# Attention groups of a twelve-stage decoder kernel: the transfers of the maxima rows issued by ScalarE instead of the sync engine

## The chip, the cores and the metric

The kernel is one program on one core of a Trainium2 chip. The metric is the device time of one execution in microseconds (us). The core has four compute engines, each with an instruction queue of its own: TensorE (PE in the profile), VectorE (DVE), ScalarE (ACT) and GpSimd (POOL). A fifth, the sync engine (SP), computes nothing and issues transfers. The engines meet only at semaphores. An engine takes its own queue in order, so whatever stands behind a wait waits too.

## The reference

The model is a decoder of four layers with three stages each, on x of 8 sequences, 256 positions and 128 features. Each stage adds f(layernorm(x)) to x. Five of the twelve stages are softmax attention with 16 heads of 8 features, and they are all that the change touches:

```python
# x: (8, 256, 128); L0a and L1a: self-attention with rotary q and k, causal
# L0x, L1x, L3x: cross-attention, keys and values from ctx_1024 (8, 256, 128)
Q, K, V = split_heads(q @ Wq + bq), split_heads(k @ Wk + bk), split_heads(v @ Wv + bv)
scores = jnp.einsum('bhqd,bhkd->bhqk', Q, K) / jnp.sqrt(8)      # causal or masked, but not in L3x
attn = jax.nn.softmax(scores, axis=-1)
attn = attn * group_prob[:, None]                               # L0x alone
x = x + jnp.einsum('bhqk,bhkd->bhqd', attn, V).merge_heads() @ Wo + bo
```

The stages run in the order L0a, L0x, L0f, L1a, L1x, L1f, L2a, L2x, L2f, L3a, L3x, L3f.

## The kernel before, in words

One function, `attention`, runs a whole group of attention stages as one pass: L0a with L0x, L1a with L1x, and L3x by itself. A pass works on items, one for each pair of stage and sequence: 16, 16 and 8 items, 40 in all. Below, items are counted from 0 to 39 over the three passes (0 to 7 are L0a, 8 to 15 L0x, 16 to 23 L1a, 24 to 31 L1x, 32 to 39 L3x).

The order of all work is written out by hand in slots. `PER` is 16 slots for each item, and the step of item i with offset `off` is done in slot 16 i + off. Each engine's program walks through the same slots and issues what falls into each, in the order of its own code. Many items are in flight at once.

What one item does, as far as it matters here:

- Slots 0 to 15: TensorE makes the scores q by k for each of 8 pairs of heads and two halves of the queries (`scores`, L714). VectorE takes each row's maximum over the keys (`row_max`, L962 and L965) into `mx`.
- Slot 16 (`MAX_CUT`): GpSimd cuts each maximum into three bf16 parts, so that a matmul can bring it in without loss (`cut_max`, L537 to L540).
- Slot 18 (`MT`): TensorE turns the parts (`turn_max`, L669). Slot 19: ScalarE copies them from PSUM to the one buffer `mT` (L890), which raises `mT_ready`.
- Slot 20 (`MAX_IN`): the sync engine waits for `mT_ready` and issues two transfers, each of 64 rows of 512 bytes, from `mT` into the operand `Qm` (L490). They raise `max_in0` or `max_in1`, by turns. ScalarE's next copy into `mT`, an item later, waits for them.
- Slots 24 to 39: TensorE makes the scores again, now keys by queries with the maxima rows as part of the operand (`keyed_scores`, L736, followed in some stages by L738 or L741 for masks). In slot 24, v = 0, it waits for both transfers. ScalarE takes the exponential in the same slot (L839) into a ring of 8 buffers `Pr`, and TensorE multiplies by the values in groups of four slots (`times_v`, L766). The keyed scores have two PSUM banks, so that TensorE in slot n waits for the exponential of slot n - 2.

So slots 16 i + 16 to 16 i + 23 of item i hold the keyed scores and exponentials of item i - 1, v = 8 to 15. In slot 20 ScalarE has the exponential with v = 12 of the item before and, for most items, one small exponential of a layernorm (L863).

The sync engine's other work in the same stretch, in the order of its code: in slot 19 the loads of the first half of the operands of item i + 2 (`stack_in`, L448: two into `Kst`, two into `Qm`, each waiting for its image in device memory); in slot 20, for L0x items, a load of the gate `G` (L474); then `MAX_IN`; in slot 21 the three writes of the k parts of item i + 3 to its image (`parts_out`, L440; 3, 2 and 1 parts of 64 KB). Masks are loaded at L465. In the first two passes GpSimd issues transfers of its own near slots 18 and 21: zeros to a buffer in device memory (L573, first pass alone) and half an expert's weights (L1500).

In slot 21 ScalarE also makes the first part of q of item i + 3 for cross-attention (`first_part`, L829), and VectorE takes the rest in slot 22 (`take_rest`, L928).

Of the kernel before, what the change touches and what calls it, by code (L numbers as in the profile page):

```python
# [36 lines left out]
DEPTH = 3  # L37
# [140 lines left out]
def load_next_weights(core, sp):  # L178

    if core.at + 1 < len(STAGES):  # L180
        st = STAGES[core.at + 1]
        sp.dma_start(core.stage_W[(core.at + 1) % 2][:, 0:width(WEIGHTS[st])], core.dram[f"small_{st}"])\
            .then_inc(core.sem["stage_w"], 16)
# [15 lines left out]
def end_pass_sync(core, sp, kind):  # L199

    sp.wait_ge(core.sem["iter_done"], 4)
    for name in ALL_STAGES + PASS_SEMS[kind]:
        sp.sem_clear(core.sem[name])  # L203
    for go in ("go_pe", "go_act", "go_dve", "go_pool"):
        sp.sem_inc(core.sem[go], 1)
# [87 lines left out]
def attention(core, sts):  # L293

    nc, s, PS, w = core.nc, core.sem, core.PS, core.w
# [18 lines left out]

    STATS, AGGR, VAR, LN, EXP, NORM = -48, -47, -46, -45, -44, -43
    XT, K, Q, V, MT, SEL, AT, Y = -38, -34, -28, 8, 18, 45, 49, 55
    MAX_CUT, MAX_IN = 16, 20
    K_CUT, Q_CUT, K_OUT, Q_OUT = -31, -25, -27, -21
    STACK_IN, FIRST_STACK_IN = (-13, -7), {"k": -22, "q": -20}
    MASK_IN, NEG, GATE_IN, XB, FFN_IN, ZERO_IN = -23, -7, 4, 45, 5, 2  # L320
# [12 lines left out]
    def slot_of(i, off):  # L333
        return PER * i + off - (LEAD[off][i] if i < 3 and off in LEAD else 0)

    def at(n, off):
        return next((i for i in range(N) if slot_of(i, off) == n), None)
# [4 lines left out]
    def unit(n, off, span=PER):  # L342
        i, r = divmod(n - off, PER)
        return (i, r) if 0 <= i < N else (None, 0)
# [3 lines left out]
    def gates(i, v, pool):  # L348
        return (10 if pool else 6) * (i - gated_from) + sum(1 for x in range(v + 1) if on_pool(x) == pool)

    def stack_slot(i, half, what):
        if i >= DEPTH:
            return PER * i + STACK_IN[half]
        return FIRST_STACK_IN[what] if i == 0 else PER * i + FIRST_STACK_IN["q"] - LEAD[Q][i]
# [5 lines left out]
    with ExitStack() as c:  # L360
# [7 lines left out]
        Qm, vaug = core.Qm, core.vaug  # L368
# [10 lines left out]
        mT = sb("mT", [P, S], BF16)  # L379
# [38 lines left out]
        with nc.Block() as block:  # L418

            @block.sync  # L420
            def _(sp):
                if first:
                    first_loads(core, sp)
                load_next_weights(core, sp)

                def parts_out(i, what, ready):

                    sp.wait_ge(s[ready], i + 1)
                    if i >= 2:
                        for half in range(2):  # L430
                            sp.wait_ge(s[f"{what}_stack{(i - 2) % DEPTH}_{half}"], 32 * ((i - 2) // DEPTH + 1))
                    out = image[what][i % 2].rearrange("s r t -> r s t")
                    if what == "k":
                        runs = ((0, 3, part["k"][:, 0:3, :]), (3, 2, part["k"][:, 0:2, :]), (5, 1, part["k"][:, 0:1, :]))
                    else:
                        three = part["q"][:, 0:1, :].broadcast_to([P, 3, S])
                        runs = ((0, 3, part["q"][:, 0:3, :]), (3, 2, part["q"][:, 0:2, :]), (5, 1, part["q"][:, 0:1, :]))
                        runs = ((0, 3, three), (3, 2, part["q"][:, 1:2, :].broadcast_to([P, 2, S])), (5, 1, part["q"][:, 2:3, :]))
                    for slot, n, src in runs:
                        sp.dma_start(out[:, slot:slot + n, :], src).then_inc(s[f"{what}_image{i % 2}"], 16)  # L440

                def stack_in(i, half, what):
                    buf, pairs = i % DEPTH, slice(half * HP // 2, (half + 1) * HP // 2)
                    sp.wait_ge(s[f"{what}_image{i % 2}"], 48 * (i // 2 + 1))
                    for par in range(2):
                        rows = image[what][i % 2].rearrange("s (r d p) t -> r s d p t", r=2, d=DH)[par][:, :, pairs, :]
                        to = Kst[64 * par:64 * par + 64, buf, pairs] if what == "k" else Qm[64 * par:64 * par + 64, buf, par, pairs]
                        sp.dma_start(to.rearrange("p h t -> p (h t)"), rows.rearrange("s d p t -> s d (p t)"))\  # L448
                            .then_inc(s[f"{what}_stack{buf}_{half}"], 16)

                for n in SLOTS:
                    i = at(n, K_OUT)
                    if i is not None:
                        parts_out(i, "k", "k_parts")
                    i = at(n, Q_OUT)
                    if i is not None:
                        parts_out(i, "q", "q_parts")
                    i = at(n, MASK_IN)
                    if i is not None and items[i][0] in MASKED:
                        st, b = items[i]  # L460
                        m = i - masked_from
                        if m > 0:
                            sp.wait_ge(s["neg_ready"], m)
                        for k in range(2):
                            sp.dma_start(msk[:, k, :, :], core.dram[f"mask{st[1]}" + "qk"[k]][b]  # L465
                                         .rearrange("(t p) k -> p t k", p=P)).then_inc(s["mask_in"], 16)
                    i = at(n, GATE_IN)
                    if i is not None and items[i][0] in GATED:
                        st, b = items[i]
                        m = i - gated_from  # L470
                        if m >= DEPTH:
                            sp.wait_ge(s["pg_dve"], gates(i - DEPTH, PER - 1, False))
                            sp.wait_ge(s["pg_pool"], gates(i - DEPTH, PER - 1, True))
                        sp.dma_start(G[:, i % DEPTH], core.dram["gate_prob"][b].rearrange("(t p) k -> p t k", p=P))\  # L474
                            .then_inc(s[f"gate_in{m % DEPTH}"], 16)
                    for half in range(2):
                        for what in "kq":
                            i = next((j for j in range(N) if stack_slot(j, half, what) == n), None)
                            if i is not None:
                                if i >= DEPTH:  # L480
                                    sp.wait_ge(s["st_psum"], PER * (i - DEPTH) + 8 * (half + 1))
                                if i == 0:
                                    sp.wait_ge(s["image_set"], 16 * 6)
                                    sp.wait_ge(s["setup"], set_up)
                                stack_in(i, half, what)
                    i = at(n, MAX_IN)
                    if i is not None:
                        sp.wait_ge(s["mT_ready"], i + 1)
                        for par in range(2):
                            sp.dma_start(Qm[64 * par + 56:64 * par + 64, i % DEPTH, par].rearrange("c p t -> c (p t)"),  # L490
                                         mT[64 * par:64 * par + 64, :]).then_inc(s[f"max_in{i % 2}"], 16)
                    if second and n == PER * (second - 1) + Y + 1:
                        sp.wait_ge(s["x_done"], second)
                        core.at += 1
                        load_next_weights(core, sp)
                        core.at -= 1
                end_pass_sync(core, sp, "attention")
                nxt = core.at + len(sts)
                sp.wait_ge(s["stage_w"], 16 * nxt)
# [320 lines left out]
            def _(act):  # L820
# [23 lines left out]
                for n in SLOTS:  # L844
# [4 lines left out]
                    i, v = unit(n, TLAG)  # L849
                    if i is not None:  # L850
                        exponentials(i, v)
                    i = at(n, LN)
# [5 lines left out]
                    i = at(n, EXP)  # L858
# [5 lines left out]
                    i = at(n, NORM + 1)  # L864
# [8 lines left out]
                    i = at(n, XT + 1)  # L873
# [5 lines left out]
                    i = at(n, K + 1)  # L879
                    if i is not None and items[i][0] not in ROPE:  # L880
                        first_part(i, "k", f_bank(K))
                    i = at(n, Q + 1)
                    if i is not None and items[i][0] not in ROPE:
                        first_part(i, "q", f_bank(Q))
                    i = at(n, MT + 1)
                    if i is not None:
                        act.wait_ge(s["mT_psum"], i + 1)
                        if i > 0:
                            act.wait_ge(s[f"max_in{(i - 1) % 2}"], 32 * ((i - 1) // 2 + 1))
                        a(mT[:, :], PS[:, f_bank(MT), 0:P].bitcast(BF16), ACT.Copy).then_inc(s["mT_ready"], 1)  # L890
                    i = at(n, AT + 1)
                    if i is not None:
                        act.wait_ge(s["aT_psum"], i + 1)
# [3 lines left out]
                    i, x = unit(n, PV_LAG + 5)  # L897
# [1684 lines left out]
```

## Time and profile before

| | |
|---|---|
| time before, median of 3 runs | 1683.09 us (1681.88 to 1686.23) |
| the profiled execution, its own time | 1681.12 us |
| span of its instructions | 1679.0 us |
| mean granted TensorE clock | 0.865 of full speed |
| busy: TensorE, VectorE, ScalarE, GpSimd | 1244.2, 981.0, 640.0, 574.5 us |

The profile is of one execution. Its span runs from the first instruction to the end of the last; the program's own time holds 2.12 us more, and is 1.97 us below the median of the three runs. Busy time of an engine is not the same as time that it sets: an engine can be idle because it waits for another, and in another stage it can be the one waited for. Transfers that the sync engine or ScalarE issues are counted at the issuing queue (SPq), and what they take to land is to be read from who waits for them.

### The profile page before, as it was taken

To read this page: it belongs to the slowest core of one execution; us is meant where nothing else is said; L and a number is where in the kernel's file an instruction comes from. 1 tells how busy PE (TensorE), PEld (TensorE's weight loads), DVE (VectorE), ACT (ScalarE), POOL (GpSimd) and SP (SyncE) were. 2 spreads that over 40 slices of the span, in tenths; PEclk is the share of its full clock that TensorE was granted. 3 is DMA by queue.
4 is the path that set the end of the run, shared out by engine and by line. 5 is a ranking of instruction groups with operands and counts; after the bars stand their busy time and mean duration, and the time that the engine had idled before them with its cause. 6 is when DMAs were issued, how large, how long until landed. Compare 5 with 4: busy or idle time off the path is not lost. (4 is left out here: it accounts for less than half of the span.)

```text
span 1679.0 us, 30784 instructions
## 1 busy us (share of the span) xinstructions
PE 1244.2 (74%) x9153; PEld 792.0 (47%) x9153; DVE 981.0 (58%) x4171; ACT 640.0 (38%) x1532; POOL 574.5 (34%) x1102
## 2 busy tenths in 40 slices
PE   4688889995293589999963947649488738995686
PEld 2455555552283356555533936538244424543232
DVE  5666777764775677787726735566333428863332
ACT  1344544542032156566541424214123314763221
POOL 3543478873332444455203433134100012310000
PEclk8899999997596699999985968859689969997888
DMA  5544654510111434554201140111100034310000
GB/s 181 162 130 141 192 170 140 159 35 15 32 56 60 149 111 137 163 166 136 76 10 40 57 152 1 44 42 55 43 0 0 0 101 131 120 48 1 0 0 25
DMA packets 139962, 137.80 MB, mean 82 GB/s; under 512 B 12240, under 2 KB 109136, under 8 KB 139552
## 3 DMA queue, kind: packets, MB, share of 16 engines
q1 hardware_dynamic: 131200, 111.40, 21.5%
q0 software_dynamic: 8608, 24.55, 4.6%
q8 instruction: 72, 1.18, 0.3%
q14 instruction: 82, 0.67, 0.1%
HBM read 84.10 MB, written 49.18 MB: 79 GB/s over the span
## 5 line engine op out<-in xcount | busy, mean ns | idle before, releaser
L839 ACT ACTIVATE L0a_Pr<-PS 128x512 f32<-128x512 f32 (+1 forms) x256 | 137.3, 547 | 153.5 <-PE PS L741 88.0
L839 ACT ACTIVATE L1a_Pr<-PS 128x512 f32<-128x512 f32 (+1 forms) x256 | 136.1, 547 | 104.8 <-PE PS L741 52.5
L557 POOL TENSOR_TENSOR L0a_PG<-L0a_Pr,L0a_G 128x512 f32<-128x512 f32 x80 | 105.8, 1327 | 29.5 <-ACT L0a_Pr L839 13.7
L962 DVE CUSTOM_DVE_ANT_0 L1a_junk<-PS,L1a_neg 128x256 bf16<-128x256 f32 x256 | 94.8, 420 | 33.7 <-PE PS L714 33.3
L962 DVE CUSTOM_DVE_ANT_0 L0a_junk<-PS,causal_q 128x128 bf16<-128x128 f32 (+1 forms) x256 | 78.5, 352 | 53.5 <-PE PS L714 52.7
L736 PE MATMUL PS<-Qm,L0a_Kst 128*128 128x512 bf16 (+1 forms) x256 | 93.2, 364 | 22.3 <-DMA Qm<-L0a_mT 19.2
L714 PE MATMUL PS<-L0a_Kst,Qm 128*128 128x256 bf16 (+1 forms) x512 | 95.1, 273 | 17.6 <-DVE L0a_mx L962 10.6
L714 PE MATMUL PS<-L1a_Kst,Qm 128*128 128x256 bf16 (+1 forms) x512 | 94.5, 271 | 16.1 <-DVE L1a_mx L962 9.2
L962 DVE CUSTOM_DVE_ANT_0 L1a_junk<-PS,causal_q 128x128 bf16<-128x128 f32 (+1 forms) x256 | 78.5, 352 | 37.4 <-PE PS L714 36.8
L736 PE MATMUL PS<-Qm,L1a_Kst 128*128 128x512 bf16 (+1 forms) x256 | 91.3, 357 | 10.8 <-DMA Qm<-L1a_mT 7.5
L965 DVE TENSOR_REDUCE L3x_mx<-PS 128x2 f32<-128x512 f32 x128 | 83.8, 686 | 22.4 <-PE PS L714 22.1
L962 DVE CUSTOM_DVE_ANT_0 L0a_junk<-PS,L0a_neg 128x256 bf16<-128x256 f32 x192 | 72.8, 418 | 35.6 <-PE PS L714 35.0
L839 ACT ACTIVATE L3x_Pr<-PS 128x512 f32<-128x512 f32 x128 | 73.1, 602 | 35.6 <-PE PS L736 35.1
L714 PEld LDWEIGHTS PS<-L0a_Kst,Qm 128*128 128x128 bf16 x512 | 44.5, 103 | 62.2 <-DVE L0a_mx L962 32.1
L714 PEld LDWEIGHTS PS<-L1a_Kst,Qm 128*128 128x128 bf16 x512 | 43.8, 102 | 60.6 <-DVE L1a_mx L962 30.4
L738 PE MATMUL PS<-neg_k,ident_b 128*128 128x256 bf16 x256 | 71.8, 280 | 0.0
L766 PE MATMUL PS<-L1a_Pr,vaug 128*32 128x256 f32 (+1 forms) x1024 | 61.7, 358 | 0.2 <-ACT L1a_Pr L839 0.2
L714 PE MATMUL PS<-L3x_Kst,Qm 128*128 128x256 bf16 x256 | 51.4, 286 | 13.9 <-DVE L3x_mx L965 9.3
L736 PE MATMUL PS<-Qm,L3x_Kst 128*128 128x512 bf16 x128 | 47.8, 381 | 5.9 <-ACT L3x_Pr L839 5.1
L741 PE MATMUL PS<-L0a_neg,ident_b 128*128 128x512 bf16 x128 | 48.5, 379 | 0.0
L741 PE MATMUL PS<-L1a_neg,ident_b 128*128 128x512 bf16 x128 | 48.5, 379 | 0.0
L2010 POOL COPY L3a_dAb<-L3a_dA 128x1024 f32<-128x1024 f32 x4 | 4.2, 1042 | 128.3 <-DVE L3a_dA L2153 128.3
(722 smaller groups left out, 3255.5 us busy)
## 6 DMA issues: line engine op xcount, KB each, us to landing
Qm<-q_image SPq DMA_DIRECT2D x160, 128.0 KB
sorted_in<-zeros POOLq DMA_DIRECT2D x16, 516.0 KB, 4.3
L0a_Kst<-k_image SPq DMA_DIRECT2D x64, 128.0 KB
ffn_w_<-L_ffn POOLq DMA_DIRECT2D x32, 256.0 KB, 4.0
L1a_Kst<-k_image SPq DMA_DIRECT2D x64, 128.0 KB
ffn_w_<-L_ffn SPq DMA_DIRECT2D x16, 256.0 KB, 7.1
L3x_Kst<-k_image SPq DMA_DIRECT2D x32, 128.0 KB
k_image<-L0a_kpart SPq DMA_DIRECT2D x16, 192.0 KB
```

The lines of the kernel that those rows point to most:

```text
L557: g.tensor_tensor(PG[:, V_ % GATED_RING, :].rearrange("p (h q) -> p h q", h=2), Pr[:, V_ % RING, :].rearrange("p (h q) -> p h q", h=2), G[ ...
L714: ins = mm(PS[:, bank, par * nk:(par + 1) * nk], Qm[:, buf, par, hp, tt * P:(tt + 1) * P], Kst[:, buf, hp, 0:nk], start=(par == 0), stop=T ...
L736: ins = mm(o, Kst[:, buf, hp, kt * P:(kt + 1) * P], Qm[:, buf, :, hp, q0:S], start=True, stop=True, **free)
L738: ins = mm(o[:, :, 0:P], core.ident_b[:, :], core.neg_k[:, :].unsqueeze(1).broadcast_to([P, 2, P]), start=False, stop=True, **free)
L741: ins = mm(o, core.ident_b[:, :], neg[:, buf, 1, kt].unsqueeze(1).broadcast_to([P, 2, S]), start=False, stop=True, **free)
L766: ins = mm(o, vaug[:, buf, half, kt, 4 * g + j, :], src[:, par * nq:(par + 1) * nq], start=(kt == 0 and half == 0), stop=True, **free)
L839: a(Pr[:, V_ % RING, 0:2 * nq], PS[:, T_BANK + v % 2, 0:2 * nq], ACT.Exp, scale=SCALE)\
L962: ins = v.tensor_tensor_reduce(junk[:, tt, par, 0:nk], scored[:, par], off, 1.0, LOWEST, ALU.add, ALU.max, mx[:, i % 2, tt, par, hp:hp + 1])
L965: ins = v.tensor_reduce(mx[:, i % 2, tt, :, hp:hp + 1], scored, AX, ALU.max)
L2010: g.tensor_copy(dAb[:, :, :, :], dA[:, :, :].unsqueeze(3).broadcast_to([P, T, NH, P]))\
```

## The change

The step `MAX_IN` of the sync engine is taken out. Its wait and its two transfers, unchanged, go into ScalarE's program, in slot MT + 2 = 20, behind that slot's exponential(s) and ahead of slot 21's. Nothing else is touched: same transfers, same semaphores, same slot number.

```diff
-    MAX_CUT, MAX_IN = 16, 20
+    MAX_CUT = 16
...
-                    i = at(n, MAX_IN)
-                    if i is not None:
-                        sp.wait_ge(s["mT_ready"], i + 1)
-                        for par in range(2):
-                            sp.dma_start(Qm[64 * par + 56:64 * par + 64, i % DEPTH, par].rearrange("c p t -> c (p t)"),
-                                         mT[64 * par:64 * par + 64, :]).then_inc(s[f"max_in{i % 2}"], 16)
...
                         a(mT[:, :], PS[:, f_bank(MT), 0:P].bitcast(BF16), ACT.Copy).then_inc(s["mT_ready"], 1)
+                    i = at(n, MT + 2)
+                    if i is not None:
+                        act.wait_ge(s["mT_ready"], i + 1)
+                        for par in range(2):
+                            act.dma_start(Qm[64 * par + 56:64 * par + 64, i % DEPTH, par].rearrange("c p t -> c (p t)"),
+                                          mT[64 * par:64 * par + 64, :]).then_inc(s[f"max_in{i % 2}"], 16)
```

## Rows read from the trace of the kernel before

**Rows 1.** Busy us by stretch (L0a, L1x, L3x): stretch, length, engines, clock, DMA share, GB/s

```profile
66.00:186.00 120.00, 99.75 (x937) 63.31 (x935) 76.60 (x464) 59.31 (x153) 53.22 (x134) 0.93 0.47 145
...
716.00:838.00 122.00, 119.90 (x1022) 67.61 (x1021) 92.82 (x491) 74.37 (x162) 51.54 (x96) 1.00 0.42 128
1413.00:1507.00 94.00, 89.67 (x803) 49.38 (x802) 71.38 (x143) 65.06 (x142) 21.61 (x68) 1.00 0.30 93
```

**Rows 2.** Line L736 on TensorE: its idle time before it by what ended it, us, times

```profile
  DMA Qm<-L0a_mT: 19.2, 8
  DMA Qm<-L1a_mT: 7.5, 7
...
  DMA Qm<-L3x_mT: 0.7, 1
```

**Rows 3.** Line L490, the sync engine's issues: ns min/median/max, first and last start

```profile
L490 SPq DMA_DIRECT2D Qm<-L0a_mT x32: 608/654/954, 55.1 to 371.5; - x32
```

**Rows 4.** Timeline of item 23 (L1a): start us, us, engine, line, [idle before <-releaser]

```profile
696.93 0.38 ACT L890 ACTIVATE L1a_mT<-PS 128x256 bf16<-128x256 bf16 x1
...
699.64 1.34 SPq L490 DMA_DIRECT2D Qm<-L1a_mT  x2
...
702.88 0.39 PE L736 MATMUL PS<-Qm,L1a_Kst 128*128 128x512 bf16 x1 [2.20 <-DMA Qm<-L1a_mT]
```

**Rows 5.** Timeline of item 29 (L1x)

```profile
806.43 0.38 ACT L890 ACTIVATE L1a_mT<-PS 128x256 bf16<-128x256 bf16 x1
...
807.67 1.34 SPq L490 DMA_DIRECT2D Qm<-L1a_mT  x2
...
812.12 0.39 PE L736 MATMUL PS<-Qm,L1a_Kst 128*128 128x512 bf16 x1 [1.47 <-DMA Qm<-L1a_mT]
```

**Rows 6.** Timeline of item 8 (L0x): the sync engine's queue and TensorE

```profile
208.87 0.45 SPq L474 DMA_DIRECT2D L0a_G<-gate_prob  x1
...
209.40 1.35 SPq L490 DMA_DIRECT2D Qm<-L0a_mT  x2
...
216.08 0.39 PE L736 MATMUL PS<-Qm,L0a_Kst 128*128 128x512 bf16 x1 [3.27 <-DMA Qm<-L0a_mT]
```

**Rows 7.** Busy us by stretch: item 8's issue to its use

```profile
209.40:216.10 6.70, 3.42 (x37) 2.12 (x36) 4.12 (x19) 2.79 (x9) 3.43 (x10) 1.00 0.96 283
```

**Rows 8.** Timeline of item 2 (L0a): all transfers issued from 89.07 on, and TensorE

```profile
89.07 1.20 SPq L448 DMA_DIRECT2D Qm<-q_image  x2
...
92.59 0.72 POOL L573 DMA_DIRECT2D sorted_in<-zeros  x1
92.89 1.34 SPq L490 DMA_DIRECT2D Qm<-L0a_mT  x2
...
98.18 0.57 PE L736 MATMUL PS<-Qm,L0a_Kst 128*128 128x512 bf16 x1 [2.22 <-DMA Qm<-L0a_mT]
```

**Rows 9.** Timeline of item 35 (L3x), the stretch around slots 19 to 24

```profile
1446.68 0.38 ACT L890 ACTIVATE L3x_mT<-PS 128x256 bf16<-128x256 bf16 x1
...
1447.09 1.34 SPq L490 DMA_DIRECT2D Qm<-L3x_mT  x2
1447.21 0.61 ACT L839 ACTIVATE L3x_Pr<-PS 128x512 f32<-128x512 f32 x1
1447.69 0.22 ACT L863 ACTIVATE L3x_r<-L3x_lnv 128x2 f32<-128x2 f32 x1
1447.78 0.62 ACT L839 ACTIVATE L3x_Pr<-PS 128x512 f32<-128x512 f32 x1
...
1448.26 0.51 ACT L829 ACTIVATE L3x_qpart<-PS,stage_W 128x256 bf16<-128x256 f32 x1
1448.54 1.46 SPq L440 DMA_DIRECT2D k_image<-L3x_kpart  x3
...
1449.43 0.38 PE L736 MATMUL PS<-Qm,L3x_Kst 128*128 128x512 bf16 x1
...
1450.31 0.38 PE L736 MATMUL PS<-Qm,L3x_Kst 128*128 128x512 bf16 x1
```

## The prediction

> **What bounds the kernel now.** I read the busy times by stretch first. In the attention passes TensorE is the engine that sets the pace: it is busy for 99.75 of 120 us in L0a (83%), 119.90 of 122 in L1x (98%) and 89.67 of 94 in L3x (95%), with ScalarE at 49%, 61% and 69% [rows 1]. The reader is to see that ScalarE has room on average, and that in L1x and L3x there is next to no idle time of TensorE left to win.
>
> Then I read what TensorE waits for at the line that uses the moved transfers, L736. It waits for them in 16 of 40 items: 19.2 us in eight items of the first pass, 7.5 in seven of the second, 0.7 in one of L3x, 27.4 us in all [rows 2]. That is the ceiling of any gain. The other 24 items use rows that have landed in time, or so nearly that no wait of note is shown.
>
> Then I read timelines, to see whether such a wait is the sync engine's lateness, the transfer's own time, or queueing. Three kinds show up.
>
> In item 23 the copy ends at 696.93 + 0.38 = 697.31, but the sync engine issues at 699.64, 2.33 us late. TensorE goes on at 702.88, 3.24 us after the issue, with 2.20 us of wait [rows 4]. In item 29 the issue is 807.67 - 806.81 = 0.86 us late, and the wait 1.47 [rows 5]. I took these starts for all 40 items: only these two issue more than 0.1 us behind the copy.
>
> In item 8 the issue is prompt, but the gate's load, issued at 208.87, stands ahead of it in the sync engine's queue. The rows are used 6.68 us after the issue, with 3.27 us of wait [rows 6], while the DMA engines are 96% busy [rows 7].
>
> In item 2 the last transfers ahead of it in that queue were issued at 89.07 and 1.20 on, over 2.6 us before the issue at 92.89. Still the rows are used only 5.29 us after it. What was issued close by is GpSimd's 92.59 [rows 8].
>
> Against these stands the landing with little in its way: at most 1450.31 - 1447.09 = 3.22 us in item 35 [rows 9], and 3.24 in item 23.
>
> **The change part by part.** Removed from the sync engine: 40 waits and 80 issues, of about 0.65 us each [rows 3], some 52 us of its queue. Added to ScalarE: the same.
>
> *Gain 1, the late issues.* ScalarE issues behind its own copy, so items 23 and 29 are no longer late. Item 23 gives back its whole 2.20 us (2.33 earlier). Item 29 gives 0.86 to 1.47; I take 1.0. Sum 3.2 us.
>
> *Gain 2, item 8.* In a queue of its own the transfer isn't behind the gate's load. Bounds 0 and 3.27 us. I take 2.0, because the DMA engines stay as full and GpSimd's transfers are still there.
>
> *Gain 3, the other waits.* In the first pass they are 19.2 - 3.27 = 15.9 us, in the second 7.5 - 2.2 - 1.5 = 3.8, in L3x 0.7. They could all go (20.4) or none. I take 1.5, by item 2, the plainest row: its own queue was clear, and the 2.05 us beyond 3.24 went to another engine's transfers. Another queue doesn't remove those.
>
> *Cost 1, the image writes move up.* With the wait for `mT_ready` gone, the sync engine goes straight to slot 21's three writes of the k parts, 384 KB (6 parts of 64 KB). In item 35 they are issued at 1448.54, directly behind the maxima's 1.34 us [rows 9]; now they start as early as or earlier than the maxima's, and compete. At the 283 GB/s seen in a full stretch [rows 7], 384 KB are 1.4 us, the most that they can put ahead; the least is 0. If the two queues share, each byte of the maxima's 64 KB waits for one of the image, 0.23 us. I take that, for the 14 items that wait and weren't late: 14 x 0.23 = 3.2 us. The 24 without a wait have slack.
>
> *Cost 2, ScalarE's queue.* Behind the two issues stand slot 21's exponential, the first part of q and slot 22's exponential; TensorE waits for the exponentials two slots on, VectorE for q. In item 35 the two issues would occupy the queue from 1447.09 to 1448.43 [rows 9]. The exponential and layernorm step of slot 20 (1447.21 and 1447.69) stand ahead of them in program order. I take it that these are already handed to the arithmetic and run on meanwhile: ScalarE's rows overlap, the next starting before the last has ended (1447.21 + 0.61 is after 1447.69), so instructions are taken ahead of the work. Then slot 21's exponential starts at 1448.43 instead of 1447.78 and ends at 1449.05, and TensorE's matmul that needs it starts at 1449.43: 0.38 us to spare. The first part of q ended at 1448.26 + 0.51 = 1448.77; 0.65 us later and with slot 22's exponential of 0.62 us behind it, that is 1450.04, before slot 24's matmul at 1450.31, which waits for it. Cost nothing, the cover being that two-slot lag. Without it, up to 0.65 us an item.
>
> The Trainium skill's page "Advanced Engine Details and Errata", section "Sequencer Loop", speaks of such a queue: engine instructions are pushed into a queue, and run on while the sequencer executes a control instruction. By it this cost is nothing, where an issue that holds up the arithmetic costs what rival A has; no row here shows ScalarE issuing a transfer.
>
> The sum: -3.2 - 2.0 - 1.5 + 3.2 + 0 = -3.5 us. Span 1679.0 - 3.5 = 1675.5. The profiled execution's own time is 2.1 more and its distance to the median 2.0, so the median goes from 1683.1 to 1679.6 us, 0.2% less. About 0.3%, 5 us, is what a measurement of this kernel can tell from no change. The forecast's own range, with gain 2 between 0 and 3.3, gain 3 between 0 and 6 and cost 1 between 0 and 6, is 1674 to 1685.
>
> **The rivals.**
>
> *A. The issue isn't hidden behind ScalarE's work (slower).* If the two issues start only when slot 20's work is done, they start in item 35 at 1447.69 + 0.22 = 1447.91, 0.82 us late. The landing, 3.22 later, is at 1451.13, 0.82 us behind today's use, and slot 21's exponential ends at 1449.25 + 0.62 = 1449.87, 0.44 us behind the matmul that needs it. The place is slot 24's matmul, the price about 0.6 us (less in items without the layernorm step), in the 14 waiting items and some 12 of L1x and L3x with under 0.5 us of slack: 26 x 0.6 = 15.6 us. Against the -3.5 that is +12: 1695 us. It decides from a delay of 0.2 us on, L3x's slack. For it speaks that no row shows such an issue; against it, the overlapping rows. A partial form, 0.3 us an item, gives +4: 1687.
>
> *B. A queue of its own removes most queueing (faster).* If the DMA engines serve a third queue's small transfers ahead of what GpSimd and the sync engine have waiting, gain 3 is two thirds of its 20.4, 13.6 us, and gain 2 is 3.3, cost 1 nothing: -20 us, 1663. A half-way form gives 1671. For it speaks item 8; against it item 2.
>
> *C. Nothing comes of it (the same).* The transfers land as they did except for the two late ones, and the image writes take back those 3.2 us: 1683. Items 2 and 35 speak for it.
>
> A rule of the Trainium skill speaks for C: "DMA: Bandwidth & Descriptors", section "Issuing engines are not separate DMA queues", says that transfers of all issuers run on the same 16 DMA engines and interleave, and that several issuers save only the time of issuing. Item 2's 5.29 us, with nothing ahead in its queue, agree. By it gains 2 and 3 would be nothing, and the sum 0.
>
> **How the numbers follow.** Chances: the forecast 0.48, A 0.21, B 0.13, C 0.18. Below 1678.0 is faster, above 1688.1 slower. Of the forecast, 0.20 fall below 1678 and 0.27 between, 0.01 above. Of A, 0.17 are slower and 0.04 same. B is faster. C is 0.02 faster, 0.14 same, 0.02 slower. That makes faster 0.35, same 0.45, slower 0.20. The range takes in the forecast's own, C, the half-way form of B and the partial form of A up to some 0.4 us an item: 1670 to 1690. Outside lie the full B (0.07) and the full A (0.11).
>
> **What the profile after would show.** Right: ScalarE's queue issues within 0.1 us of the copy's end in all 40 items, items 23 and 29 lose their waits, item 8's falls under 1.5 us, TensorE's total wait for these rows is 20 to 25 us, and TensorE's waits for ScalarE's exponentials at L736 stay about as they are. The image writes are issued before or beside the maxima's. Wrong by A: issues 0.3 us or more behind the copy, new waits in L3x, exponentials of slot 21 that end after their matmul could start. Wrong by B: the total wait under 12 us. The prediction would also fail if an issue on ScalarE takes much longer than 0.65 us, for then the two slots no longer cover it.

## The result: slower, outside the predicted range

| | before | after |
|---|---|---|
| median, runs side by side on one chip | 1683.09 us (1680.24 to 1686.82, 5 runs) | 1708.81 us (1704.42 to 1716.94, 5 runs) |
| ratio after to before, 95% interval | | 1.0131 [1.0104, 1.0159] |
| the profiled execution, own time | 1681.12 us | 1716.94 us |

The change costs 25.7 us in the median. The prediction was 1679.6 with a range to 1690. The profiled execution of the changed kernel is the longest of its five, 8.1 us above their median, so its parts are first sorted by place. In the changed kernel the lines stand six lower: L736 is L730, L839 is L833, L890 is L884; ScalarE's new issues are L889.

The page of the changed kernel, its span, its busy times and two of its DMA queues:

```profile
span 1715.1 us, 30784 instructions
...
PE 1267.3 (74%) x9153; PEld 808.3 (47%) x9153; DVE 980.3 (57%) x4171; ACT 638.0 (37%) x1532; POOL 572.8 (33%) x1102
...
q1 hardware_dynamic: 125440, 108.78, 20.9%
...
q10 hardware_dynamic: 5760, 2.62, 0.6%
```

The work is the same, and q10 is a queue that the page of before doesn't have: 2.62 MB, which are 80 transfers of 64 rows of 512 bytes. ScalarE's transfers do have a queue of their own.

The stretches from the first item's copy into `mT` to the last item's, for each of the three passes (stretch, length, busy us of TensorE, its weight loads, VectorE, ScalarE and GpSimd, TensorE's clock, DMA share, GB/s). Before:

```profile
55.12:370.85 315.73, 281.52 (x2695) 170.82 (x2694) 224.07 (x1061) 156.49 (x369) 203.63 (x353) 0.97 0.46 143
577.94:842.68 264.74, 247.85 (x2247) 147.67 (x2246) 197.26 (x1116) 155.25 (x369) 116.22 (x254) 0.99 0.42 131
1400.03:1508.21 108.18, 101.44 (x888) 54.66 (x886) 82.30 (x168) 74.25 (x163) 25.86 (x82) 1.00 0.30 92
```

After:

```profile
55.29:382.22 326.93, 286.82 (x2694) 173.14 (x2693) 223.55 (x1061) 155.70 (x369) 203.08 (x353) 0.95 0.45 138
588.03:860.39 272.36, 249.35 (x2247) 147.59 (x2246) 196.64 (x1116) 154.41 (x369) 116.06 (x254) 0.98 0.42 126
1426.96:1539.31 112.35, 103.77 (x888) 56.20 (x886) 82.23 (x168) 74.13 (x163) 25.88 (x82) 0.97 0.30 90
```

The passes are longer by 11.2, 7.6 and 4.2 us, 23.0 together, of which 13.9 are idle time of TensorE (length less busy: 34.2, 16.9 and 6.7 became 40.1, 23.0 and 8.6) and 9.1 are the same matmuls taking longer. The profiled span is 36.1 us longer, and the rest lies where nothing was edited: 9.2 us between the second and the third pass (566.57 against 557.35, at a clock of 0.77 instead of 0.79) and 5.0 behind the last copy (175.8 against 170.8, at 0.82 instead of 0.84), less 1.1 us elsewhere. The four other executions have spans of 1702.5 to 1707.1 us, so they hold little of this. I put the change's cost at the 23 to 26 us that passes and medians show.

TensorE's waits for the moved transfers (total, times, longest), to be held against [rows 2]:

```profile
PE PS L730 <- DMA Qm<-L0a_mT: 23.7, 8, 3.8
PE PS L730 <- DMA Qm<-L1a_mT: 14.0, 12, 2.4
...
PE PS L730 <- DMA Qm<-L3x_mT: 3.0, 3, 2.5
```

They were 27.4 us in 16 items and are 40.7 in 23. That is 13.3 of the 13.9 us of idle time. TensorE's wait for exponentials of the first pass at the same line rose from 3.1 to 4.8 us, in the two later passes it stayed (3.1 and 5.1).

ScalarE's new issues, ns min/median/max:

```profile
L889 ACTq DMA_DIRECT2D Qm<-L0a_mT x32: 623/625/2373, 55.3 to 382.9; - x32
L889 ACTq DMA_DIRECT2D Qm<-L1a_mT x32: 623/624/1131, 588.1 to 861.1; - x32
L889 ACTq DMA_DIRECT2D Qm<-L3x_mT x16: 623/624/1139, 1427.0 to 1540.0; - x16
```

The median is that of the sync engine [rows 3]; the maximum isn't.

Item 21 shows what happens. It is an item that hardly waited before (timeline; start, us):

```profile
664.86 0.38 ACT L890 ACTIVATE L1a_mT<-PS 128x256 bf16<-128x256 bf16 x1
...
665.26 1.34 SPq L490 DMA_DIRECT2D Qm<-L1a_mT  x2
...
666.72 2.52 SPq L440 DMA_DIRECT2D k_image<-L1a_kpart  x3
...
668.44 0.39 PE L736 MATMUL PS<-Qm,L1a_Kst 128*128 128x512 bf16 x1
```

The same item after:

```profile
677.12 1.43 SPq L440 DMA_DIRECT2D k_image<-L1a_kpart  x3
...
677.96 0.38 ACT L884 ACTIVATE L1a_mT<-PS 128x256 bf16<-128x256 bf16 x1
...
678.37 0.62 ACTq L889 DMA_DIRECT2D Qm<-L1a_mT  x1
...
678.59 0.47 SPq L465 DMA_DIRECT2D L1a_msk<-mask1q  x1
...
679.02 0.73 ACTq L889 DMA_DIRECT2D Qm<-L1a_mT  x1
679.10 0.94 SPq L465 DMA_DIRECT2D L1a_msk<-mask1k  x1
...
680.91 1.22 SPq L448 DMA_DIRECT2D L1a_Kst<-k_image  x2
682.23 1.19 SPq L448 DMA_DIRECT2D Qm<-q_image  x2
...
683.85 0.39 PE L730 MATMUL PS<-Qm,L1a_Kst 128*128 128x512 bf16 x1 [2.41 <-DMA Qm<-L1a_mT]
```

Before, the sync engine stood in front of its wait for `mT_ready` until the copy ended, and everything behind that wait came after the maxima. After, three image writes are issued 1.22 us before the copy ends (677.12 against 678.34), the two mask loads come between and beside ScalarE's issues, and four operand loads follow before the rows are used. The rows are used 5.51 us after the copy (683.85 - 678.34) instead of 3.20 (668.44 - 665.24). The prediction's list of what moves up had the image writes alone; the masks and the operand loads were missing.

### The profile page after: what moved, and what is told of

It is laid out like the page before. It is cut to its first block and busy times, and to the rows that moved or that the text cites. A ratio compares the mean times of both kernels' runs of the same rounds, so it can differ in the third digit from the quotient of the medians.

```text
span 1715.1 us, 30784 instructions
## 1 busy us (share of the span) xinstructions
PE 1267.3 (74%) x9153; PEld 808.3 (47%) x9153; DVE 980.3 (57%) x4171; ACT 638.0 (37%) x1532; POOL 572.8 (33%) x1102
## 3 DMA queue, kind: packets, MB, share of 16 engines
q10 hardware_dynamic: 5760, 2.62, 0.6%
## 5 line engine op out<-in xcount | busy, mean ns | idle before, releaser
L833 ACT ACTIVATE L0a_Pr<-PS 128x512 f32<-128x512 f32 (+1 forms) x256 | 136.8, 546 | 172.0 <-PE PS L735 89.8
L833 ACT ACTIVATE L1a_Pr<-PS 128x512 f32<-128x512 f32 (+1 forms) x256 | 135.8, 547 | 120.5 <-PE PS L732 63.5
L730 PE MATMUL PS<-Qm,L0a_Kst 128*128 128x512 bf16 (+1 forms) x256 | 94.5, 369 | 28.5 <-DMA Qm<-L0a_mT 23.7
L730 PE MATMUL PS<-Qm,L1a_Kst 128*128 128x512 bf16 (+1 forms) x256 | 91.6, 358 | 17.3 <-DMA Qm<-L1a_mT 14.0
L962 DVE CUSTOM_DVE_ANT_0 L0a_junk<-PS,L0a_neg 128x256 bf16<-128x256 f32 x192 | 72.7, 418 | 36.5 <-PE PS L708 36.1
L833 ACT ACTIVATE L3x_Pr<-PS 128x512 f32<-128x512 f32 x128 | 73.1, 601 | 40.5 <-PE PS L730 40.2
L730 PE MATMUL PS<-Qm,L3x_Kst 128*128 128x512 bf16 x128 | 49.1, 391 | 8.2 <-ACT L3x_Pr L833 5.1
```

Source lines behind the costliest of these rows:

```text
L730: ins = mm(o, Kst[:, buf, hp, kt * P:(kt + 1) * P], Qm[:, buf, :, hp, q0:S], start=True, stop=True, **free)
L833: a(Pr[:, V_ % RING, 0:2 * nq], PS[:, T_BANK + v % 2, 0:2 * nq], ACT.Exp, scale=SCALE)\
L962: ins = v.tensor_tensor_reduce(junk[:, tt, par, 0:nk], scored[:, par], off, 1.0, LOWEST, ALU.add, ALU.max, mx[:, i % 2, tt, par, hp:hp + 1])
```

## The experiments

Each is compared with the kernel before, run on the same chip in between (medians 1686.4 to 1687.2 us). "Landing" is the time from the end of item i's copy to the semaphore update of the second transfer, read from each trace; the means are over the eight items 1 to 8 and the seven items 33 to 39. Before, they are 5.50 and 3.03 us; in the changed kernel 6.36 and 3.12. Waits and landings are those of one profiled execution of each kernel.

The expectations name theories by letters. W: the sync engine's transfers, no longer held back, are what costs. Q: ScalarE's queue is served worse. E: ScalarE's exponentials come late. S: the transfers of two issuers at one time delay each other. D: it is the bytes, from whichever queue. G: the loss needs GpSimd's transfers as a third party.

| kernel | time, us | ratio, 95% interval | waits for the rows | landing 1–8 | 33–39 |
|---|---|---|---|---|---|
| changed + sync waits for the copy | 1705.79 | 1.0112 [1.0092, 1.0131] | 40.4 | 6.45 | 3.19 |
| changed + sync waits for the landing | 1684.71 | 0.9989 [0.9971, 1.0007] | 26.1 | 5.51 | 3.02 |
| before, image writes first | 1715.32 | 1.0166 [1.0140, 1.0192] | 50.6 | 6.33 | 3.34 |
| before + spares on ScalarE | 1717.57 | 1.0183 [1.0163, 1.0204] | 54.0 | 6.34 | 4.14 |
| before + one-row spares on ScalarE | 1692.03 | 1.0036 [1.0008, 1.0063] | 32.6 | 5.59 | 3.17 |
| before + spares two slots later | 1685.52 | 1.0002 [0.9979, 1.0025] | 27.3 | 5.51 | 3.06 |
| before + spares on the sync engine | 1694.81 | 1.0051 [1.0027, 1.0074] | 32.4 | 5.64 | 3.13 |
| before, GpSimd's transfers moved | 1658.42 | 0.9821 [0.9799, 0.9843] | 10.4 | 3.67 | 3.04 |
| changed, GpSimd's transfers moved | 1668.23 | 0.9882 [0.9851, 0.9914] | 16.4 | 4.04 | 3.01 |
| the same + sync waits for the landing | 1656.35 | 0.9813 [0.9787, 0.9839] | 11.6 | 3.90 | 3.02 |

### The changed kernel, with the sync engine held until the copy

```diff
+                    i = at(n, MT + 2)
+                    if i is not None:
+                        sp.wait_ge(s["mT_ready"], i + 1)
```

> The changed kernel, but the sync engine still waits for the maxima's copy in slot 20 before it goes on to the image writes; it issues nothing there. Theory W (the k parts' image writes, which the old wait held back until after the maxima's issues, now go first and fill the DMA engines): the writes can start at the copy's end at the earliest, so that items 21, 22, 32 and those of L1x, where they moved up by 1.2 us and more ahead of the copy, get their landing back to within 0.5 us of before, and items 1 to 4 and 17 to 20, where they moved to about the copy's end in any case, stay. About a third to a half of the loss comes back: 1695 to 1700 us. Theory Q (ScalarE's queue is served worse than the sync engine's, whatever else goes on): nothing comes back, 1705 to 1712 us. Theory E (ScalarE's exponentials come late): nothing comes back either.

It keeps the wait in the sync engine's program and leaves the transfers on ScalarE, so the image writes start 0.03 us after the copy's end, at the same moment as ScalarE's issues. 1705.79 us: it gives back little, less than the third to a half that theory W had forecast. In the first two passes, what goes *beside* the maxima in another queue costs as much as what goes ahead of them (landings of 6.45 us in items 1 to 8 against 6.36). L3x gets its time back, with waits of 1.0 us where the changed kernel has 3.0.

L3x also shows how little the image writes cost by themselves. In items 33 to 36 of this run nothing but the three image writes, 384 KB, is issued by the sync engine from the copy's end until 2.78 us after it, and they start at the same moment as ScalarE's issues. The rows land 3.09, 3.53, 3.32 and 3.31 us after the copy, on the mean 0.28 us later than before the change. (Item 32, the first of the pass, lands 1.1 us later; its second issue is late too.) The same writes beside them go with 0.95 us in items 1 to 8, where GpSimd's transfers are on their way too.

### The changed kernel, with the sync engine held until the landing

```diff
+                    i = at(n, MT + 2)
+                    if i is not None:
+                        sp.wait_ge(s[f"max_in{i % 2}"], 32 * (i // 2 + 1))
```

> The changed kernel, but the sync engine waits in slot 20 until the maxima's transfers have landed, so that no image write is issued while they are on their way. Theory W: landings as before the change or better, TensorE's wait for these rows at or below the 27 us of before, 1675 to 1684 us. Theory Q: landings stay late in busy stretches, 1700 us or more. Theory E: no change, 1705 to 1712 us. If the writes come too late for the loads that need them, new waits for the stacks at L708 would show.

The transfers are still issued by ScalarE, in its queue, in all 40 items. The waits (this kernel's L733; L3x no longer appears):

```profile
PE PS L733 <- DMA Qm<-L0a_mT: 19.2, 8, 3.8
...
PE PS L733 <- DMA Qm<-L1a_mT: 6.9, 9, 2.2
```

The whole loss is gone: 1684.71 us, a ratio of 0.9989 with an interval that holds 1. So neither ScalarE's issuing nor its queue costs the time by itself; the sync engine's transfers do that it no longer holds back. This is the run that settles the main cause, although the time is 0.7 us above the range of theory W. It doesn't tell image writes from masks and loads, since it holds all of them. It also holds them longer than the kernel before did, until the landing and not only until the issue, and no run holds the kernel before for as long; a small cost of ScalarE's issues that this makes up for isn't excluded here.

### The kernel before, with the image writes ahead in the same queue

```diff
-                    i = at(n, K_OUT)
-                    if i is not None:
-                        parts_out(i, "k", "k_parts")
...
+                    i = at(n + 1, K_OUT)
+                    if i is not None:
+                        parts_out(i, "k", "k_parts")
                     i = at(n, MAX_IN)
```

> The kernel before, with the sync engine's three image writes of the k parts put ahead of the maxima's wait and transfers instead of behind them; ScalarE issues nothing. It is the change's second effect, the writes moved up, without its first, the other issuer. Theory W (the moved writes are what costs): the rows land about 1.3 us later where the k parts are ready just before the copy (L0a, L1a), less in L1x and L3x; the wait at L736 grows from 27 to 45 us or more, 1700 to 1712 us. Theory S (what costs is that two engines issue at one time, whatever they issue): one queue, so no more than the issues' own delay, about 0.6 us in items 1 to 8 and 17 to 24, 1688 to 1697 us.

Item 3 of it:

```profile
118.21 0.38 ACT L890 ACTIVATE L0a_mT<-PS 128x256 bf16<-128x256 bf16 x1
...
118.38 1.43 SPq L440 DMA_DIRECT2D k_image<-L0a_kpart  x3
...
119.86 2.12 SPq L490 DMA_DIRECT2D Qm<-L0a_mT  x2
...
124.72 0.39 PE L736 MATMUL PS<-Qm,L0a_Kst 128*128 128x512 bf16 x1 [3.04 <-DMA Qm<-L0a_mT]
```

With ScalarE out of it altogether, the order alone costs 28.2 us (1715.32 against 1687.16), 3 us more than the range of theory W and far from that of theory S. Here a part of the price is plain to see as a late issue: 119.86 is 1.27 us after the copy's end. Counted from its own first issue the transfer takes no longer than before in items 1 to 8 (5.47 us on the mean against 5.48). From the copy's end it is 6.33, against 6.36 in the changed kernel, where the issue is prompt and the transfer is longer. In the first pass the writes that go ahead cost 0.83 to 0.86 us an item, whether the maxima stand behind them in one queue or share the DMA engines with them from another.

### Spare transfers on ScalarE, on the sync engine, smaller, and later

The kernel before keeps its order, and ScalarE issues two more transfers of the same 64 rows into a tile that nobody reads, in slot 20; ScalarE's next copy into `mT` waits for them too.

```diff
+                    i = at(n, MT + 2)
+                    if i is not None:
+                        act.wait_ge(s["mT_ready"], i + 1)
+                        for par in range(2):
+                            act.dma_start(spare[64 * par + 56:64 * par + 64].rearrange("c p t -> c (p t)"),
+                                          mT[64 * par:64 * par + 64, :]).then_inc(s["dum_in"], 16)
```

> The kernel before, with two more transfers of the same size and source issued by ScalarE in slot 20, into a spare buffer that nobody reads; the real ones stay with the sync engine. It adds the occupation of ScalarE's queue (80 issues) and 64 KB an item, and leaves the image writes where they were. Theory E (the issues on ScalarE cost by themselves): slower by 10 us or more. Theory W: within 0.3% of before, 1679 to 1688 us, the real rows landing up to 0.2 us later. Theory Q says nothing of it, but the spare transfers' landings would be late.

1717.57 us, as slow as the changed kernel and more. That is what theory E had forecast and theory W hadn't. Item 37 lies in a stretch of L3x in which no other transfer is issued until 2.78 us after the copy:

```profile
1506.99 0.38 ACT L892 ACTIVATE L3x_mT<-PS 128x256 bf16<-128x256 bf16 x1
...
1507.39 1.34 SPq L491 DMA_DIRECT2D Qm<-L3x_mT  x2
1507.40 0.65 ACTq L897 DMA_DIRECT2D L3x_spare<-L3x_mT  x1
1508.08 0.62 ACTq L897 DMA_DIRECT2D L3x_spare<-L3x_mT  x1
...
1511.43 0.39 PE L737 MATMUL PS<-Qm,L3x_Kst 128*128 128x512 bf16 x1 [0.65 <-DMA Qm<-L3x_mT]
```

The real rows, issued 0.02 us after the copy's end, are used 4.06 us after it. With no spares they land 3.04 us after it. So 64 KB more, started at the same moment by another engine, put 1.0 us onto a transfer that has the DMA engines nearly to itself otherwise.

Most of that isn't time in which the rows' data are moved. By the trace's records of single packets, the last data packet of the real rows ends 2.69, 2.70 and 2.29 us after the copy in items 37 to 39, where it ended at 2.29, 2.31 and 2.23 before. The last semaphore update comes 1.33, 1.60 and 1.58 us behind that packet, and came 0.75, 0.74 and 0.73 us behind it before. No run shows what fills that time.

This run alone can't say whether ScalarE's 1.3 us of issuing has a part in it. The same two transfers in slot 22 (`MT + 4` in place of `MT + 2`) answer that:

> The two whole spare transfers on ScalarE again, issued in slot 22 instead of 20, some 2 us after the real ones. Theory S: the real rows are issued and nearly landed by then, landing in L3x back to 3.0 us, and the time within 0.5% of before, 1680 to 1693 us; what stays comes from the image writes and loads behind. Theory E: as slow as with slot 20, or slower, since the exponential of slot 23 is nearer to its use: 1710 us or more.

```profile
1482.11 0.38 ACT L892 ACTIVATE L3x_mT<-PS 128x256 bf16<-128x256 bf16 x1
...
1482.52 1.34 SPq L491 DMA_DIRECT2D Qm<-L3x_mT  x2
...
1483.74 1.30 ACTq L897 DMA_DIRECT2D L3x_spare<-L3x_mT  x2
...
1485.74 0.38 PE L737 MATMUL PS<-Qm,L3x_Kst 128*128 128x512 bf16 x1
```

ScalarE's queue is held for the same 1.3 us, the real rows land after 3.06 us again, and the kernel takes 1685.52 us, no more than before (the interval reaches to 0.25%, 4 us). TensorE's waits for exponentials at the line of the keyed scores are 2.1 us longer than before, 13.4 against 11.3, but a cost of ScalarE's queue time can't be told in the kernel's time. Theory E, which had 1710 us or more here, falls.

The spares cut to one row of 512 bytes each (`spare[64 * par + 56:64 * par + 57, 0, :]` from `mT[64 * par:64 * par + 1, :]`):

> As the run with two spare transfers on ScalarE, but each moves one row of 512 bytes instead of 64. Theory S by descriptors (the making of the descriptors of both issuers' transfers is one shared step, whose time goes with their number): the real rows land as before the change, in L3x 3.0 us after the copy, and the time is within 0.3% of before, 1680 to 1690 us. Theory S by transfers (a fixed time for each transfer): the landing stays at 4.0 us, and 1705 to 1718 us. Theory E (ScalarE's queue is what costs): the exponentials come late as with the whole spare transfers only if an issue still takes 0.6 us.

1692.03 us, 2 us above the forecast range, and landings of 3.1 to 3.2 us in L3x. The number of transfers is the same, so most of the cost goes with what is in them. The 4.9 us that are left weren't followed up.

And the full spares issued by the sync engine, right behind the real ones:

> The same two spare transfers, issued by the sync engine directly behind the real ones: same bytes, one queue. Theory S: the real rows' landing stays within 0.2 us of before (3.0 in L3x), 1680 to 1692 us. Theory D (it is the bytes on the DMA engines that delay, from whichever queue): landings 0.3 us and more later, over 1695 us.

1694.81 us, with 3.1 to 3.2 us in L3x. The landing is what theory S had forecast, the time is 3 us above its range, and the waits are 5 us longer than before; the sync engine is busy with 80 more issues, and which of its later work comes late by them wasn't looked into.

Behind in the same queue, the same bytes cost the real rows 0.1 us; beside them in another queue, 1.0. But that is not the queue alone. Behind the real ones, the spares are issued 1.4 us after the copy. The spares two slots later are in the other queue and are issued 1.25 us after the copy (1483.74 against 1482.49), and they cost the rows nothing either. In L3x, then, what protects the rows is the head start of some 1.3 us. One queue gives it by its order, since the two issues ahead take 0.65 us each. In two queues that wait for the same copy it is gone.

### GpSimd's transfers out of the way

What made items of the first pass wait in the kernel before? GpSimd's zeros and weights were moved in their slots, with and without the change:

```diff
-    MASK_IN, NEG, GATE_IN, XB, FFN_IN, ZERO_IN = -23, -7, 4, 45, 5, 2
+    MASK_IN, NEG, GATE_IN, XB, FFN_IN, ZERO_IN = -23, -7, 4, 45, 14, 12
```

> The kernel before, with GpSimd's two transfers of an item (zeros, half an expert's weights) issued in slots 12 and 14 of an item instead of 2 and 5, which are slots 18 and 21 of the item before. If the waits for the maxima rows before the change were queueing behind these, most of the 27.4 us of wait go: TensorE's wait at L736 for the rows under 10 us in all, and 1655 to 1668 us. If they only move the collision to the operand loads of slots 3 and 9, waits for the stacks at L714 grow and the time stays at 1675 to 1690 us.

```profile
PE PS L736 <- DMA Qm<-L1a_mT: 5.0, 5, 2.4
...
PE PS L736 <- DMA Qm<-L0a_mT: 4.5, 4, 1.9
...
PE PS L736 <- DMA Qm<-L3x_mT: 0.9, 1, 0.9
```

1658.42 us, 28.0 us less than the kernel before beside it, within the forecast range, and waits of 10.4 us instead of 27.4. The first pass is 22.4 us shorter (293.36 against 315.73). Items 2 to 5 land after 3.05 to 3.09 us. Most of the queueing that the change was up against was GpSimd's, and a change of issuer didn't touch it.

> The changed kernel with GpSimd's transfers of the two items of pass 1 moved twelve and ten slots on, as in the run of the kernel before with the same move (1658.4 us). Theory W (the changed kernel lets the sync engine's image writes go ahead of the maxima's transfers, and theory S, that the two issuers' transfers delay each other) has nothing to do with GpSimd: the change should cost here what it cost in the kernel before, 15 to 25 us on top of 1658.4, so 1673 to 1685 us, with landings at 4 to 6 us after the copy in most items. Rival G (the loss needs GpSimd's transfers as a third party): the change costs under 5 us here, 1655 to 1663 us, landings near 3.1 us.

(The moves are nine slots for the weights and ten for the zeros, as the diff has them, and not the twelve and ten of the text above.) With the change on top it is 1668.23 us. The change costs 9.8 us here instead of 25.7 (10.4 by the two ratios, as the two kernels ran on different chips), less than either way of 15 to 25 that I had expected, and more than 5. Landings in items 1 to 8 are 0.37 us later than without the change, where they were 0.86 later with GpSimd's transfers in place. So the sync engine's transfers cost some time by themselves, and more where three engines' transfers meet.

> The changed kernel in which the sync engine waits for the landing of the maxima's transfers before it goes on, with GpSimd's transfers moved as well. By theory W nothing of the sync engine's overlaps the maxima's transfers, so landings are 3.0 to 3.2 us after the copy in nearly all items, the late issues of items 23 and 29 are gone too: 1650 to 1660 us. If holding the sync engine for some 3 us an item makes its own image writes and loads late once the queueing is gone, it is 1660 to 1672 us, with waits for K or V images among those of TensorE.

1656.35 us, which can't be told from the 1658.42 without the change: the intervals of their ratios overlap almost wholly. Item 23 lost most of its late issue's wait (1.85 us became 0.14), but items 24 and 29 wait 1.88 and 1.70 us in its place. No form of the change was shown to gain anything; moving GpSimd's transfers alone was.

## Why the prediction was wrong

**The step that failed is Cost 1.** It named the right mechanism, with an upper bound, and then took 0.23 us for 14 items, 3.2 us. Measured: the waits rose by 13.3 us, though items 23 and 29 gave back 0.70 and 1.47, so the others lost 15.5. Three things were wrong in it.

- *The price by bytes.* 64 KB at 283 GB/s are 0.23 us. That is near what the image writes cost in the quiet stretch of L3x (0.28 us, the run in which the sync engine waits for the copy), but only one of the 14 priced items, item 32, lies in L3x. The mean over items 1 to 8 of the changed kernel was 0.86, and with GpSimd's transfers moved 0.37. Nor is it a price for all transfers: the spares put 64 KB beside the rows and cost 1.0 us with almost nothing else moving. The bound of 1.4 us was no bound either: in item 21 the use came 2.31 us later after the copy than before.
- *The items.* "The 24 without a wait have slack" is false: 23 items wait now where 16 did, and item 29 no longer does, so eight of the 24 lost their slack. Item 21 is one.
- *What moves up.* The wait for `mT_ready` held back everything behind it in the sync engine's program, the masks too, and the operand loads behind them, not just the image writes of slot 21.

A further term wasn't in the sum at all. After item 5's wait of 3.76 us the profile shows TensorE at the lower of its clock levels (columns as above):

```profile
158.50:162.35 3.85, 0.09 (x3) 0.01 (x1) 1.46 (x10) 0.75 (x3) 1.93 (x4) 0.80 0.85 258
162.35:166.00 3.65, 3.65 (x18) 2.23 (x22) 1.51 (x10) 1.22 (x3) 0.00 (x0) 0.50 0.60 196
...
170.00:173.70 3.70, 3.48 (x36) 2.12 (x36) 1.71 (x10) 1.09 (x4) 0.09 (x1) 1.00 0.00 0
```

It was all but idle for 3.85 us, then runs at 0.50 of full speed, 1.2 GHz, and is back at 1.00, 2.4 GHz, by 170. The matmul at 162.35 takes 0.61 us, one of the same shape at full speed 0.39. In the three passes TensorE's busy time for the same work rose by 5.3, 1.5 and 2.3 us, 9.1 in all. By the trace's record of the clock, the lower level covers 33.8 us of the first pass instead of 19.3, 9.7 instead of 5.0 of the second and 6.8 instead of none of L3x. In the first pass it comes with the waits of items 1, 2, 4, 5, 7 and 8, in L3x with that of item 32. Items 17 to 24 wait 1.2 to 2.4 us each without such a fall. So some of the longer waits were paid once as idle time and once more as slow matmuls. How much of the 9.1 us is due to the change isn't settled: the changed kernel with the sync engine held until the landing has shorter waits than the kernel before, and 4.5 us more of TensorE's busy time in the same passes. The row of item 2 in [rows 8] had shown such a matmul (0.57 us behind a wait of 2.22), and I didn't price it.

**Gain 1** was half right. Item 29 lost its wait of 1.47 us. Item 23 is issued 0.03 us after the copy instead of 2.33, yet waits 1.50 instead of 2.20: it met the sync engine's loads and writes.

```profile
713.58 0.38 ACT L884 ACTIVATE L1a_mT<-PS 128x256 bf16<-128x256 bf16 x1
...
713.98 0.62 ACTq L889 DMA_DIRECT2D Qm<-L1a_mT  x1
...
714.62 1.19 SPq L448 DMA_DIRECT2D Qm<-q_image  x2
...
718.82 0.39 PE L730 MATMUL PS<-Qm,L1a_Kst 128*128 128x512 bf16 x1 [1.50 <-DMA Qm<-L1a_mT]
```

**Gain 2**, 2.0 us for a queue without the gate's load ahead, was 0.6 us of loss: item 8 waits 3.82 us instead of 3.27. **Gain 3** was a loss as well, by the means above.

**Cost 2** was right, nearly to the end. ScalarE issues 0.03 us behind the copy in all 40 items. The exponentials that were handed over before run on meanwhile. Item 6 shows that, and the exception:

```profile
177.57 0.65 ACTq L889 DMA_DIRECT2D Qm<-L0a_mT  x1
177.70 0.40 ACT L833 ACTIVATE L0a_Pr<-PS 128x256 f32<-128x256 f32 x1
...
178.25 2.37 ACTq L889 DMA_DIRECT2D Qm<-L0a_mT  x1
180.72 0.38 ACT L833 ACTIVATE L0a_Pr<-PS 128x256 f32<-128x256 f32 x1 [2.54 <-issue]
...
181.16 0.28 PE L730 MATMUL PS<-Qm,L0a_Kst 128*128 128x256 bf16 x1 [1.30 <-ACT L0a_Pr L833]
```

The exponential at 177.70 runs during the issue. But the second issue took 2.37 us there, in a stretch full of other engines' transfers, and what stood behind it was late. Issues of over 1 us stand in items 5 to 8 and in the first item of each pass; the waits for exponentials rose by 1.7 us. The prediction had named an issue of more than 0.65 us as what would break the cover.

**The sum.** By its own bounds (gain 2 from 0 to 3.3 us, gain 3 and cost 1 each from 0 to 6) the forecast's own range would have been 1671 to 1686 and not 1674 to 1685. The measured 1708.81 lies outside of both.

**The rivals.** A came out on the right side, slower, but not by its mechanism: issues were prompt and L3x had no delay from them, and in the run with spares two slots later no cost of ScalarE's queue time could be told. B is refuted: 40.7 us of waits against its 12. C fell with Cost 1. The Trainium skill's page "DMA: Bandwidth & Descriptors", section "Issuing engines are not separate DMA queues", which I had cited for C, says that several issuers save the issuing time and no more; the runs agree that nothing else was saved. The section "Queues, rings and completion order" of the same page of the Trainium skill has each DMA engine serve its queues by turns. It is a reason for a *loss* that I had read past. The spares agree with it in so far as the real rows' data packets end up to 0.4 us later with spares beside them in another queue; the larger part of the 1.0 us stands behind the last data packet, and turns between queues don't explain that.

**What stays open.** How the 0.86 us an item divide among image writes, masks and loads. Whether the spares' 1.0 us goes with their 128 rows or with the few partitions that they are read from and written to, which are those of the real rows; one row each of the same partitions cost 0.1 to 0.2, and six times as many bytes to device memory, the image writes in L3x, 0.28. And why GpSimd's transfers more than double the cost of the change.

## What to carry to other kernels

Before a transfer with its wait is taken out of a queue, list what that wait holds back: an in-order wait is also a head start for what stands behind it first, and a second queue that waits for the same event gives it away. Price a transfer that others run beside from rows in which such transfers meet, in as full a stretch, and not from bytes over bandwidth: here the price was 0.3 us in a quiet stretch and 0.9 in a full one. Where a wait shows queueing, look first for whose transfers are queued; here moving those by some slots was worth 28 us, and moving the victim to another issuer cost 26.

## What the runs showed of the hardware that I had not expected

- Two pairs of 64-row transfers, started together by the sync engine and ScalarE with almost nothing else moving (items 37 to 39): the pair that is waited for lands 3.9 to 4.3 us after the copy instead of 3.0, though its last data packet ends 0.1 to 0.4 us later only. With a second pair that starts 1.3 to 1.4 us later, from the same engine or the other: 3.0 to 3.2.
- Three image writes, 384 KB, started together with the rows by another engine in items 33 to 36 of L3x: 0.06 to 0.50 us on the landing.
- An issue on ScalarE takes 0.62 us, but up to 2.37 us in a full stretch.
- Three image writes ahead of the maxima cost items 1 to 8 of the first pass about 0.85 us each, by one queue (6.33 against 5.50) or by two (6.36).
